# Flamingo layer on one core: scores with tokens on the partitions, and a new order of each quad's work

## What is computed

```python
x = x + jnp.tanh(g_xattn[0]) * xattn(layernorm(x), ctx_1024, mask, Wq, bq, Wk, bk, Wv, bv, Wo, bo)
x = x + jnp.tanh(g_ffn[0]) * ffn(layernorm(x), gate_w, w1, w2)

# ffn
probs = jax.nn.softmax(jnp.einsum('ntd,ed->nte', x, gate_w), axis=-1)
g, m = jax.lax.top_k(probs.transpose(0, 2, 1), k)
h = jax.nn.gelu(jnp.einsum('nekd,edf->nekf', x[batch_idx, m], w1), approximate=False)
h = jnp.einsum('nekf,efd->nekd', h, w2)
out = zeros.at[batch_idx, m].add(g[..., None] * h)
```

## Time and profile before

| | us |
|---|---|
| median of 3 runs (lowest, highest) | 1564.37 (1562.61, 1566.11) |
| profiled execution, its own time | 1563.59 |
| its span in the trace | 1561.8 |
| TensorE busy | 1493.4 (96%) |
| VectorE busy | 1015.7 (65%) |
| ScalarE busy | 732.8 (47%) |
| GpSimd busy | 593.7 (38%) |
| mean granted TensorE clock | 0.987 of full |

### The profile page before, as it was taken

How to read it: one execution, slowest core, us unless ns; L and a number is a source line. 1 busy time by engine, 2 the same in 40 slices (tenths; PEclk the granted TensorE clock), 3 DMA queues, 4 the chain that set the end, 5 groups by cost and what they waited for, 6 DMA issues and landing times.

```text
span 1561.8 us, 22316 instructions
## 1 busy us (share of the span) xinstructions
PE 1493.4 (96%) x7169; PEld 1211.2 (78%) x7169; DVE 1015.7 (65%) x1716; ACT 732.8 (47%) x1347; POOL 593.7 (38%) x554
## 2 busy tenths in 40 slices
PE   6886699999999999999999999999999999999996
PEld 5654477787788888888888888888888888888885
DVE  2578776657766676676657676767667675766542
ACT  1385233445444554454445444455445444554432
POOL 2265555543544044323443244403531444323211
PEclk9999699999999999999999999999999999999998
DMA  7176423543333333245234423334324433442133
GB/s 229 55 255 204 162 88 99 141 138 82 89 120 62 101 97 95 93 88 116 82 108 81 110 91 99 74 95 103 100 76 95 110 96 93 82 108 81 42 78 70
DMA packets 101401, 163.58 MB, mean 105 GB/s; under 512 B 7411, under 2 KB 45315, under 8 KB 101285
## 3 DMA queue, kind: packets, MB, share of 16 engines
q1 hardware_dynamic: 86885, 128.50, 26.4%
q0 software_dynamic: 14400, 33.56, 11.9%
HBM read 128.48 MB, written 33.55 MB: 104 GB/s over the span
## 4 chain that ended last, share of the span: by engine, by line
PE 86%; DVE 7%; issue 2%; ACT 2%; POOL 1%; DMA 1%; POOLq 0%; SPq 0%; DVEq 0%; ACTq 0%
PE bank L1325 42%; PE bank L1211 33%; PE bank L1185 4%; PE bank L1480 2%; PE bank L572 1%; PE bank L590 1%; PE bank L400 1%; DVE st L817 1%; DVE onehot L1366 1%; ACT xT L641 1%; DVE sc L793 0%; DMA ctx_raw<-in_ctx 0%; PE bank L1355 0%; DVE w2hl L1170 0%; DVE hid_low L1203 0%
## 5 line engine op out<-in xcount | busy, mean ns | idle before, releaser
L1325 PE MATMUL bank<-w2hl,hh 128*128 128x512 f32 x2048 | 635.7, 392 | 0.0
L1211 PE MATMUL bank<-xo,whl 128*128 128x512 f32 x2352 | 543.0, 390 | 3.7 <-DVE mix L1275 2.8
L1211 PEld LDWEIGHTS bank<-xo,whl 128*128 128x128 f32 x2352 | 440.7, 188 | 98.5 <-DVE mix L1275 3.7
L1325 PEld LDWEIGHTS bank<-w2hl,hh 128*128 128x128 f32 x2048 | 380.4, 188 | 76.0
L1325 PE MATMUL bank<-w2hl,hid_low 128*128 128x512 f32 x1024 | 398.7, 389 | 0.0
L1325 PEld LDWEIGHTS bank<-w2hl,hid_low 128*128 128x128 f32 x1024 | 192.2, 188 | 40.4
L1430 POOL DMA_INDIRECT layer_out<-y,slot_row x64 | 103.2, 1613 | 301.8 <-ACT y L1345 287.0
L1170 DVE TENSOR_TENSOR w2hl<-raw,w2hl 128x512 fp32r<-128x512 f32 x213 | 147.7, 715 | 50.6 <-ACT w2hl L1165 41.3
L1139 POOL TENSOR_TENSOR whl<-raw,whl 128x512 fp32r<-128x512 f32 x56 | 82.1, 1466 | 258.2 <-ACT whl L1105 258.2
L1165 ACT ACTIVATE w2hl<-raw 128x512 fp32r<-128x512 f32 x228 | 136.5, 624 | 60.1 <-DMA raw<-in_L_ffn_w 43.9
L1144 POOL TENSOR_TENSOR whl<-wsum,whl 128x512 fp32r<-128x512 f32 x56 | 75.1, 1341 | 183.4 <-ACT whl L1126 183.4
(11 more groups left out here) (224 smaller groups left out, 1783.0 us busy)
## 6 DMA issues: line engine op xcount, KB each, us to landing
raw<-in_L_ffn_w SPq DMA_DIRECT2D x228, 256.0 KB, 2.7
raw<-in_L_ffn_w SPq DMA_DIRECT2D x72, 512.0 KB, 4.9
x_s<-in_x SPq DMA_DIRECT2D x8, 1024.0 KB, 6.9
layer_out<-x SPq DMA_DIRECT2D x8, 1024.0 KB, 9.0
xn_rows<-xn SPq DMA_DIRECT2D x8, 1024.0 KB, 4.9
raw_k<-in_L_xattn_Wk SPq DMA_DIRECT2D x1, 1024.0 KB, 5.4
raw_q<-in_L_xattn_Wq SPq DMA_DIRECT2D x1, 1024.0 KB, 11.3
raw_v<-in_L_xattn_Wv SPq DMA_DIRECT2D x1, 1024.0 KB, 13.4
```

Of the source, the lines that this page charges most:

```text
L1211: last = pe.matmul(bk[:, :], whl[:, p % 2, part, 2 * w + k, :], xo[:, xpart, x, k, :], start=(not adds and k == 0 and part == HIGH and xpa ...
L1325: last = pe.matmul(Y_BANKS[c][:, :], high if hpart == HIGH else low[:, c * P:(c + 1) * P], w2hl[:, f % 4, part, :], start=(s == 0 and hpar ...
```

## The change

Scores: the stationary operand is now 128 tokens of `xT`, the moving one `qkc`, which has one more column (-1/512, so that the same matmul gives minus the mean of x; JM = 86). They come out with tokens on the partitions, into one of two banks; the copy `sT` and the turn back are gone, and the turns of x have two banks instead of three. `vg` has a ninth column of ones, so that the router matmul gives the sums of the exponentials. The maximum is subtracted on VectorE (L783), and one instruction takes the exponentials of a quad. ScalarE no longer sums x. From quad 4 on VectorE's weighing sums x1 as it goes, and ScalarE takes the squares; the statistics instructions stay for quads 0 to 3.

TensorE computes the scores a quad ahead, and the first two quads' turns stand ahead of preparation part 1. VectorE starts a quad with its softmax. The choice starts in quad 4, with five places a quad, and it is finished, with `hot_dve` and `slots_dve`, in quad 6. GpSimd gathers ahead of the normalising of quad 6; w1's first split comes after that. ScalarE squares the last quad and splits the first weights ahead of the tokens.

```diff
-            spare = onehot[:, :, :].rearrange("p (q t) s -> p q (t s)", q=Q)
+        spare = overlay("spare", [P, 2, Q, D], BF16)
...
-        T_BANKS = (2, 3, 4)
+        T_BANKS = (2, 3)
         O_BANKS = (bank[0], bank[1])
-        VG_BANK, SC_BANK, CHOICE_BANK = bank[5], bank[6], bank[7]
-        CHOOSE_FROM, PLACES = QB + 1, 3
+        SC_BANKS = (bank[6], bank[4])
+        VG_BANK, CHOICE_BANK = bank[5], bank[7]
+        CHOOSE_FROM, PLACES = QB, 5
...
+        def score(pe, q, i):
+
+            if i == 0:
+                wait(pe, mean_ready, q - 1)
+                wait(pe, sc_ready, q - 1)
+            pe.wait_ge(turn_out, turn_at["x", q, i] + 1)
+            for k in range(KD):
+                last = pe.matmul(SC_BANKS[q % 2][:, i * JM:(i + 1) * JM], xT[:, q % 2, k, i * P:(i + 1) * P],
+                                 qkc[:, k, q // QB, :], start=(k == 0), stop=(k == KD - 1))
...
+            wait_evacuated(pe, step_at["mean", 0])
+            pe.wait_ge(tails, 2 * B)
+            for i in range(Q):
+                turn_x(pe, 0, i)
+            for i in range(Q):
+                score(pe, 0, i)
+            for i in range(Q):
+                turn_x(pe, 1, i)
+            prep_pe(pe, 1)
+            for q in range(NQ):
+                if q + 1 < NQ:
+                    for i in range(Q - 1):
+                        score(pe, q + 1, i)
+                turn_e(pe, q)
+                if q + 1 < NQ:
+                    score(pe, q + 1, Q - 1)
+                if q == 0:
+                    wait_evacuated(pe, len(steps) - 1)
+                route(pe, q)
+                between(q, 0)
+                for i in range(Q - 1):
+                    weigh_pe(pe, q, i)
+                between(q, 1)
+                weigh_pe(pe, q, Q - 1)
+                between(q, 2)
+                for i in range(Q):
+                    if q + 2 < NQ:
+                        turn_x(pe, q + 2, i)
+                    if i == 1:
+                        between(q, 3)
+                between(q, 4)
...
+            for q in range(NQ):
+                exps(q)
+                e_out(q)
+                if q == CHOOSE_FROM:
+                    choice_act(act, 0)
+                if q - 1 >= LATE:
                     for i in range(Q):
+                        square_x1(q - 1, i)
+                if LEAD <= q + 1 < NQ:
                     for i in range(Q):
+                        square(q + 1, i)
+                if q + 2 < NQ:
                     for i in range(Q):
+                        x_out(q + 2, i)
+            for i in range(Q):
+                square_x1(NQ - 1, i)
+            w1_high_act(act, 0, 0, 0)
...
-                if it == NQ:
-                    w1_low_pool(pool, 0, 0, 0)
+                if it == NQ - 1:
                     for c in range(NC):
                         gather_pool(pool, 0, 0, c)
+                if it == NQ:
                     promote_pool(pool, 0, 0)
+                    w1_low_pool(pool, 0, 0, 0)
...
+            router_in(0)
+            prep_out(dve, prep_dve, False, 1, own)
+            for q in range(NQ):
+                softmax_in(q)
+                if q >= 2 and q - 2 != CHOOSE_FROM - 1:
+                    logits_out(q - 2)
+                if 1 <= q <= LATE:
+                    stats(q - 1, range(Q))
+                    moments(q - 1)
+                between(q, 0)
+                if q + 1 < NQ:
+                    router_in(q + 1)
+                weights_in(q)
+                weigh(q, 0)
+                if q == CHOOSE_FROM:
+                    logits_out(q - 1)
+                    choice_start_dve(dve, own, 0)
+                weigh(q, 1)
+                between(q, 1)
+                weigh(q, 2)
+                between(q, 2)
+                weigh(q, 3)
+                if q >= LATE:
+                    mean_out(q)
+                between(q, 3)
+                between(q, 4)
+            logits_out(NQ - 2)
+            for c in range(NC):
                 split_tokens_dve(dve, 0, c)
             logits_out(NQ - 1)
...
-            act.wait_ge(scored, NQ)
+            for c in range(NC):
+                first_tokens_act(act, c)
             for f in range(2):
                 w2_high_act(act, 0, 0, f)
             w1_high_act(act, 0, 0, 1)
-            for c in range(NC):
-                first_tokens_act(act, c)
```

More of the change, by code:

```diff
@@ new lines, in turn_e, with route @@
+        def turn_e(pe, q):
+            pe.wait_ge(exped, q + 1)
+            pe_bank_free(pe, ("e", q, 0))
+            for i in range(Q):
+                last = pe.transpose(turn_bank(("e", q, 0))[0:J, i * P:(i + 1) * P], ex[:, q % 2, i, :], ident[:, :])
+            last.then_inc(turned, 1)
+        def route(pe, q):
+            pe.wait_ge(turn_out, turn_at["e", q, 0] + 1)
+            wait(pe, rinv_ready, q)
+            for i in range(Q):
+                last = pe.matmul(VG_BANK[:, i * EM:(i + 1) * EM], eT[:, q % 2, i * P:(i + 1) * P], vg[:, q // QB, :],
+                                 start=True, stop=True)
+            last.then_inc(routed, 1)
@@ new lines, in weigh_pe @@
+        def weigh_pe(pe, q, i):
+            n = Q * q + i
+            wait(pe, added, n - 1)
+            pe.matmul(O_BANKS[n % 2][:, :], eT[:, q % 2, i * P:(i + 1) * P], vo[:, q // QB, :],
+                      start=True, stop=True).then_inc(weighed, 1)
+        def attention_pe(pe, between):
+            wait_evacuated(pe, step_at["mean", 0])
[23 more added lines that the diff above has]
+                between(q, 2)
+                for i in range(Q):
+                    if q + 2 < NQ:
[3 more added lines that the diff above has]
+                between(q, 4)
@@ L824, in attention_dve, with stats @@
-            for c in (0, 1):
+                                         op0=ALU.mult, op1=ALU.add,
+                                         accum_out=x1sum[:, q % 2, i:i + 1] if q >= LATE else None)\
+                   .then_inc(added, 1)
+            def stats(q, tiles):
+                if tiles[0] == 0 and q >= 1:
+                    dve.wait_ge(x1_stats, q)
+                for i in tiles:
+                    dve.wait_ge(added, Q * q + i + 1)
+                    own.mark(dve.bn_stats(st2[:, i, :], x1[:, q % 2, i, :]))
@@ new lines, in moments, with mean_out @@
+            def moments(q):
+                dve.wait_ge(dve_own, own.n)
+                for i in range(Q):
+                    last = dve.bn_aggr(mv2[:, q % 2, i, :], st2[:, i, :])
+                    own.mark(last) if i < Q - 1 else last.then_inc(x1_stats, 1)
+            def mean_out(q):
+                dve.wait_ge(added, Q * q + Q)
+                dve.tensor_scalar(x1mean[:, q % 2, :], x1sum[:, q % 2, :], -1.0 / D, None, ALU.mult)\
+                   .then_inc(x1_mean, 1)
+            router_in(0)
@@ L870, in step @@
                 dve.wait_ge(dve_own, own.n)
-            if b == 0 and piece == 0:
-                choice_start_dve(dve, own, 0)
             if piece == 0:
@@ L1828, in _ @@
             pool.memset(mean_m[:, :], 1.0 / D).then_inc(consts, 1)
+            for b in range(B):
+                pool.memset(qkc[:, :, b, JE:JM], -1.0 / D).then_inc(tails, 1)
+                pool.memset(vg[:, b, E:EM], 1.0).then_inc(tails, 1)
             pool.wait_ge(pool_start, 4)
```

381 lines of the change are left out of this document (158 added, 223 removed).

## The result

Five runs of each kernel on one chip: 1569.84 us (1567.13 to 1571.12) against 1562.74 before (1562.60 to 1566.11), a ratio of 1.0039 with a 95% interval of 1.0027 to 1.0051. The forecast of 1560 was wrong, and the time lies above its range, which ended at 1568. The other 2.7 us stand in executions that no profile shows.

The account below looks back on a forecast made before the run. TensorE was taken to bound quads 0 to 2, VectorE the choice, then a chain, with only the first expert matmul's start moving. Terms -2.0 - 3.0 - 11.8 + 2.0 + 9.5 + 1.0 = -4.3 us gave 1560; range from just under 1553 to 1568.

Parts of the forecast that it names:

- start, first result of quad 0: Kernel start: first weighed result of quad 0 at 61.1 instead of 63.16 us, 2.0 us earlier.
- quads 0 to 2: TensorE sets the pace in the first three quads; each takes 10.7 us, 1.0 less, so 3.0 less in all.
- choice quads to the slots, with the clock: Stretch from quad 3's first result to slots ready: 11.8 us less, with 2.0 given back for TensorE's lower clock.
- slots to the expert matmul: End of attention: a whole quad now stands behind the slots, 20.9 us against 11.4, so 9.5 more.
- from there to expert 1's first product: First expert: the second choice's first piece starts later against TensorE, which waits for its count; 1.0 us more.
- the count's wait: TensorE's wait in the first hidden block for the second choice's first count: 1.0 us more, bounds 0 to 2.
- the 0.11 taken from the weight loads: Quad scores on TensorE: 32 records at 0.11 us, the spacing of 128-column weight loads, 3.55 us; bound 2.3.
- rival (a): Turned scores: loads hide behind the columns, 0.07 us a record, 0.9 less at eight places, 1553 us; chance 0.15.
- Rival (c): Quads stay at 11.7 us because VectorE's softmax waits for GpSimd; no gain there, 1563 us; chance 0.20.
- (b): TensorE stays at 2.4 GHz: nothing lost in quads 5 and 6, 3.8 less at the end, 1554 us; chance 0.13.
- Rival (d): TensorE falls to 1.2 GHz at the choice's first piece and stays; quads 4 to 6 lose 12.5, 1570 us; chance 0.12.
- the 0.1 taken from ScalarE's squares: VectorE's weighings that also sum their row: 0.1 us more each, bounds nothing and 0.19.

Follow-up runs that it names:

- b56: Kernel before the change plus 14 tiny unused TensorE products (56 instructions) at the very start: 1567.8 us, ratio to before 1.0029.
- b128: Kernel before the change plus 32 tiny unused TensorE products (128 instructions) at the very start: 1560.43 us, ratio to before 0.9988.
- a200: Changed kernel plus 50 tiny unused TensorE products (200 instructions) at the very start: 1565.49 us.
- a136: Changed kernel plus 34 tiny unused TensorE products (136 instructions) at the very start: 1564.62 us.
- a72: Changed kernel plus 18 tiny unused TensorE products (72 instructions) at the very start: 1563.91 us, ratio to before 1.0009.
- a72n: a72 with three steps moved: GpSimd's last deviations before w1's low half, VectorE's last logits between token splits, ScalarE's exponential before w2 copies: 1561.06 us.
- u1: a72 with the gather of the first expert's tokens put back behind GpSimd's normalisation of quad 6: 1570.41 us.
- c1: a72 with ScalarE's w1 high half and first token copies before the last quad's squares, second choice's exponential before w2 copies: 1558.01 us, ratio to before 0.9971.

## Why the prediction was wrong, by its own steps

| term | forecast | trace |
|---|---|---|
| start, first result of quad 0 | -2.0 | 58.88 for 63.16: -4.3 |
| quads 0 to 2 | -3.0 | 33.47 for 35.15 us: -1.7 |
| choice quads to the slots, with the clock | -9.8 | 64.97 for 73.54: -8.6 |
| slots to the expert matmul | +9.5 | 21.36 for 11.32: +10.0 |
| from there to expert 1's first product, at 369.39 (before 371.05) | +1.0 | 190.71 for 187.88: +2.8 |
| on to the first branch | 0 | 340.5 for 339.05: +1.5 |
| four turns of the loop | 0 | 677.0 for 672.4: +4.6 |
| sum | -4.3 | +4.4 |

**The step that failed** stands in the paragraph on what bounds the kernel: "the change touches nothing there: whatever is gained or lost is the time at which the first expert matmul (L1185) starts, 183.17 now". The first expert matmul started nearly as early as forecast (178.68 for 178), and the time still rose. No instruction of the loop was touched, but the place of the loop in TensorE's code was, since the scores' new form has more records. Of the 8.7 us between -4.3 and +4.4, 4.6 are this, shown by b56, b128, a200, a136 and a72. The rest is 1.8 of the count's wait, 1.5 of the clock ahead of the first branch, and 0.8 of the attention. Nor was the 3.5 to 3.9 us branch in the profile of before looked at; it was hidden there, behind products still in the queue.

**The count's wait** was the right mechanism with too small a size: 1.0 with bounds 0 to 2, and it is 2.8 with all that hangs on it. The forecast gives no working for its 1.0. It did not count that TensorE now starts when VectorE still has three logit operations, the maximum and the subtraction ahead of it, which before lay in a wait for tokens.

**The +1.5 ahead of the first branch** is the clock. From 409.3 to 412.7 us, before and after:

```profile
409.30:412.70 3.40, 3.22 (x20) 2.31 (x21) 2.81 (x6) 1.41 (x3) 0.00 (x0) 1.00 0.00 0
```

```profile
409.30:412.70 3.40, 3.40 (x24) 2.44 (x23) 1.67 (x4) 1.89 (x3) 0.00 (x0) 0.50 0.02 5
```

TensorE is granted 1.2 GHz (0.50 of full) for these 3.4 us, 1.5 us after it had idled 1.79 us in one piece for VectorE in expert 1 (from 406.0 to 407.8). It idles 1.79 us at the same place in the kernel before, and is not slowed. The stretch shows in a200, a136, a72n and u1, not in a72, c1, b56 and b128. Why a given execution has it was not settled, nor tried.

**The attention** was read well in sum, -4.5 where -5.3 was forecast, in part by luck. The start gained 4.3 where 2.0 was forecast, but 2.0 of that are not the change. One step of the preparation, 32 records that both kernels have, took longer in the profiled execution of the kernel before (first row) than in that of the changed kernel:

```profile
15.75 6.43 PE L400 MATMUL bank<-ctxT,wkT 128*128 128x154 f32 x32 [0.89 <-ACT wkT L455]
```

```profile
15.08 4.44 PE L404 MATMUL bank<-ctxT,wkT 128*128 128x154 f32 x32 [0.89 <-ACT wkT L459]
```

It took 6.43, 6.56 and 6.29 us in before, b56 and a72n, and 4.44 in the other seven profiled executions, with the change or without it. In the first three the trace's first record of the granted clock, at full, starts at 19.8 to 20.1 us, in the others at 13.4 to 15.4; the view by stretches, which gives 1.00 ahead of the first record too, does not show it. So the change itself gave about 2 at the start, as forecast (2.3 here without those 2.0; 2.1 from b128's 61.74 to a72's 59.62). And a72n, with the same program up to the last quad, had its first result at 61.98 where a72 had it at 59.62.

The score records stand 0.11 apart (32 from 30.68 to the next row's start at 34.22), so the 0.11 taken from the weight loads was right and rival (a) falls. (Its price was too low as well: 3.55 less 2.3 is 1.25 a place, and it takes 0.9.) The quads came 10.98, 10.97 and 11.52 apart against the 10.7 that was forecast; a72, a136, a200, a72n, u1 and c1 have 10.97 to 10.99 three times, so the third was slow in this execution only, and a quad gains 0.7 instead of 1.0. Rival (c), no gain there, falls too. Slots were ready at 157.3 for 157 forecast, with a granted clock of 0.90 and 0.84, so (b) falls. That the slots' time agrees is luck: what the start had too much, the quads and the choice had too little (-14.6 in all for -14.8 forecast).

Rival (d), TensorE down to 1.2 GHz in the choice, did not hold in this execution. It names 1570 us, but by a path that the trace does not show. In two of the seven profiled executions with the change, a200 and a72n, it is seen for one stretch: the scores that stand ahead of quad 6's results run at half the clock (0.50 granted from 137 to 143 us). First a72, then a72n:

```profile
137.45 2.89 PE L563 MATMUL bank<-qkc,xT 128*128 128x86 f32 x24
```

```profile
140.23 5.40 PE L563 MATMUL bank<-qkc,xT 128*128 128x86 f32 x24
```

The first result of quad 6 then comes 16.4 us after the last of quad 5 instead of 13.0. A time that agrees is not a mechanism that agrees.

**The accumulator.** A read of its own, 0.08 us, stands behind each summing operation. It starts 0.67 after its operation, and the next result starts 0.09 later still (125.12, 125.79, 125.88). So the Trainium skill, "VectorE: DVE Perf Modes", section "Two Vector instructions with no wait between them", was right that it is a second instruction, and the 0.1 taken from ScalarE's squares was the right price.

What stays open: 2.7 of the 7.1 us between the medians. The slow scores ahead of quad 6's results are of that size, but no profile shows whether the slower executions of the changed kernel had them. Open is also why the 32 records of the preparation are slow in some executions. b128's first result comes at 61.74 and not at 63.16 as before, and the 32 records above (4.44 for 6.43) account for that; its span is 2.2 us shorter than before's, 1.3 of it in the loop and 1.4 there, less 0.5 elsewhere. Only the 1.3 belongs to the place of the loop.

## What to carry to other kernels

Before a change is priced, ask what it does to the place of each loop in its engine's code, and read three rows for it: the branch's duration, the packets of the instruction queue, and "issue" as the releaser of the first work of a turn. If a loop nearly fits, a few harmless instructions ahead of it are worth trying before anything else, and they must be set again after every edit ahead of the loop; two versions of a kernel are compared fairly only with the loop placed alike. And before a difference between two traces is put down to the change, look whether a stretch that both kernels share took the same time in each: here 2.0 us of the gain at the start did not come from the change. And where a start is moved forward on one engine, follow the chain on the engine that feeds its second wait, not only its first: a gain at the start is worth what that chain can follow.

## What the runs showed of the hardware

- The same loop of 1693 instructions took 167.79 us a turn with its branch at 0.22 us and no fetch of code (b128, a72), 167.8 to 168.6 with fetches that mostly came in time (before, a136, a200), and 168.7 to 170.0 with fetches that came late (b56 and the changed kernel). What was varied in these runs is only where in a piece of code the loop begins.
- Branches of 3.3 to 4.5 us cost TensorE almost nothing of themselves: products already queued cover them (before: branch from 710.1 to 714.0, next products at 714.35), and a136 has a turn of 167.79 us with a branch of 3.39. What costs is the second piece, where at most 36 instructions of the first are left behind the branch's target.
- A summing VectorE operation costs 0.09 us more, in a read of its own of 0.08.
- FP32 records with a stationary operand of 128 columns and 86 moving columns stand 0.11 us apart, as the weight loads of 128 columns do in the earlier trace rows. The moving columns alone, at the 0.43 us of 512, would give 0.07.
- The same four gathers land 8.2 us after their issue (median) at the end of the last quad, with the DMA engines 0.87 busy, and 3.6 ahead of it, with 0.61. Whether the one comes of the other was not tried.
- The same instructions can differ by some us from one execution to the next: 32 records of the preparation took 6.43 or 4.44 us, and 24 score records ahead of quad 6's results 5.40 at a granted clock of 0.50 or 2.89 at 1.00.
